# Order of the first key products and the router's transposes, and twelve products ahead of the first layer

## The reference

```python
def _L0_xattn_ref(Q, K, V):                  # Q = layernorm(x), K = V = ctx
    x = einsum('bdn,bdm->bnm', Q, K) / sqrt(dk)
    return einsum('bvn,bnm->bvm', V, sigmoid(x))
def _L0_ffn_ref(h, router_weight, ...):      # h = layernorm(x)
    logits = h @ router_weight.T + router_bias
    # top 4 of 16 experts, softmax; gate_up and down projections of all experts, weighted
def _L3_xattn_ref(h, cond=ctx, ...):         # much later
    kvx = einsum('bsi,oi->bso', cond, w_kv_x)
    kx = _ln(kx.reshape(b, sc, g, d), kxln_w, kxln_b)
x = x + _L0_xattn_ref(_layernorm(x), ctx_2048, ctx_2048)
x = x + _L0_ffn_ref(_layernorm(x), ...)
```

## Time and profile before

| what | value |
|---|---|
| median of 3 runs | 1107.0 us (1106.76 to 1107.4) |
| profiled execution | 1105.54 us |
| its span | 1103.5 us |
| PE busy | 1025.0 us (93%) |
| PEld busy | 869.4 us (79%) |
| DVE busy | 874.6 us (79%) |
| ACT busy | 622.6 us (56%) |
| POOL busy | 567.3 us (51%) |
| mean granted clock of TensorE | 0.986 |

### The profile page before, as it was taken

The page is one execution under the profiler, slowest core; times in us unless marked ns, Lnnn a source line. Parts: engine busy times, 40 slices in busy tenths (PEclk is TensorE's granted clock), DMA queues, the critical chain, the costliest instruction groups (busy, mean ns, idle before and its releaser), DMA issues.

```text
span 1103.5 us, 19047 instructions
## 1 busy us (share of the span) xinstructions
PE 1025.0 (93%) x6546; PEld 869.4 (79%) x6546; DVE 874.6 (79%) x2154; ACT 622.6 (56%) x1657; POOL 567.3 (51%) x412
## 2 busy tenths in 40 slices
PE   6999999999998899888878899999999999999988
PEld 5458888888887686556556888998889988999976
DVE  6448777776778956589999888888887898888885
ACT  1584344444333346677747566666767667765643
POOL 3146666668653243043435665646565475655640
PEclk9999999999999999989979999999999999999999
DMA  7003111110100010100000101010000101000201
GB/s 267 1 1 110 32 55 52 35 59 29 58 1 27 1 56 18 61 1 2 20 1 19 59 1 39 1 58 2 21 19 1 59 1 39 1 20 1 88 1 39
DMA packets 15007, 37.43 MB, mean 34 GB/s; under 512 B 1648, under 2 KB 6848, under 8 KB 14400
## 3 DMA queue, kind: packets, MB, share of 16 engines
q1 hardware_dynamic: 14912, 36.21, 9.7%
HBM read 35.16 MB, written 1.05 MB: 33 GB/s over the span
## 4 chain that ended last, share of the span: by engine, by line
PE 64%; DVE 23%; ACT 6%; issue 4%; POOL 2%; DMA 0%; DVEq 0%; SPq 0%; ACTq 0%; POOLq 0%
PE bank L737 15%; PE bank L759 8%; PE bank L2153 7%; PE bank L2176 7%; PE bank L2084 7%; PE bank L2059 3%; ACT y L2301 3%; PE bank L2095 3%; PE bank L1119 2%; DVE y L286 2%; DVE bst L249 2%; DVE g_ql L2018 2%; PE bank L2073 1%; PE bank L527 1%; DVE arena L1618 1%
## 5 line engine op out<-in xcount | busy, mean ns | idle before, releaser
L2301 ACT ACTIVATE y<-bank,g_mx 128x256 f32<-128x256 f32 x256 | 117.5, 486 | 97.6 <-DVE g_mx L2464 97.6
L2579 POOL TENSOR_TENSOR y<-y,g_sm 128x1024 f32<-128x1024 f32 x64 | 120.2, 1898 | 24.0 <-DVE g_sm L2477 24.0
L2555 POOL TENSOR_TENSOR g_c<-arena 128x1024 fp32r<-128x1024 f32 x30 | 64.1, 2137 | 116.3 <-DVE arena L2398 116.3
L2176 PE MATMUL bank<-arena 128*128 128x256 f32 x512 | 116.0, 379 | 0.0
L788 ACT ACTIVATE arena<-arena 128x512 f32<-128x512 f32 x64 | 40.5, 634 | 120.4 <-DVE arena L873 120.4
L2176 PEld LDWEIGHTS bank<-arena 128*128 128x128 f32 x512 | 94.9, 190 | 12.0 <-issue 0.2
L737 PE MATMUL bank<-b_yh,b_wh 128*128 128x512 f32 x256 | 100.6, 393 | 0.0
L737 PE MATMUL bank<-b_yl,b_wh 128*128 128x512 f32 x256 | 100.0, 391 | 0.0
L737 PE MATMUL bank<-b_yh,b_wl 128*128 128x512 f32 x256 | 99.7, 389 | 0.0
L2059 PE MATMUL bank<-cst,y 128*128 128x128 f32 x512 | 74.0, 277 | 17.7 <-DVE x L2386 14.6
L824 POOL TENSOR_TENSOR b_hl<-arena,b_hh 128x512 fp32r<-128x512 f32 x64 | 81.3, 1292 | 9.6 <-ACT b_hh L797 9.6
(11 more groups left out here) (384 smaller groups left out, 3153.4 us busy)
## 6 DMA issues: line engine op xcount, KB each, us to landing
arena<-in_dram SPq DMA_DIRECT2D x37, 512.0 KB, 3.5
arena<-in_dram SPq DMA_DIRECT2D x18, 256.0 KB, 3.9
arena<-in_dram SPq DMA_DIRECT2D x3, 1024.0 KB, 5.1
arena<-in_dram SPq DMA_DIRECT2D x2, 704.0 KB, 7.0
x<-in_dram SPq DMA_DIRECT2D x4, 256.0 KB, 5.5
cx<-in_dram SPq DMA_DIRECT2D x4, 256.0 KB, 5.6
cxT<-in_dram SPq DMA_DIRECT2D x4, 256.0 KB, 5.8
cx<-in_dram SPq DMA_DIRECT2D x1, 1024.0 KB, 6.1
```

The costliest lines, as they stand in the source:

```text
L2176: m = pe.matmul(o[:, st * 256:st * 256 + 256], g_t[:, c, st * P:st * P + P], keys, start=True, stop=True)
L2301: m = act.activation(g_p[:, c, st, :], o[:, st * 256:st * 256 + 256], ACT.Exp, bias=g_mx[j % 2][:, 2 * c + st:2 * c + st + 1], accum_out=g ...
L2555: pool.tensor_tensor(cat, g_o[j % 2], g_om, ALU.subtract).then_inc(s_gc, 1)
L2579: pool.tensor_tensor(pf, pf, sums, ALU.mult).then_inc(s_gp, 1)
```

## The change

On TensorE, twelve products of `mhalf` with itself (128 by 128 by 128) go into the first quarter of the bank of batch 0's scores, ahead of those scores; nobody reads them, and the scores overwrite them. They wait for `s_pool` to reach 1.

On TensorE at the start of stage B, key product 0 now stands between the transposes of batch 0 and those of batch 1, product 1 between those of batch 1 and batch 2, and the first logits follow the transposes of batch 2. ScalarE's order is changed accordingly. On GpSimd both halves of the key weights are centred in a row, ahead of batch 1's reciprocal root, which stood between them.

```diff
@@ A_pe
                     o = claim(pe, ("A", "s", b))
+                    if b == 0:
+                        pe.wait_ge(s_pool, 1)
+                        for _ in range(12):
+                            pe.matmul(o[:, 0:P], mhalf[:, :], mhalf[:, :], start=True, stop=True)
                     pe.wait_ge(s_ctx[b], 16)
@@ B_pe
-            yt_pe(pe, K_B, "B", range(3))
+            yt_pe(pe, K_B, "B", (0,))
+            K_raw_pe(pe, 0)
+            yt_pe(pe, K_B, "B", (1,))
+            K_raw_pe(pe, 1)
+            yt_pe(pe, K_B, "B", (2,))
             logits(0)
-            K_raw_pe(pe, 0)
-            K_raw_pe(pe, 1)
             yt_pe(pe, K_B, "B", (3,))
@@ B_act
-            yt_act(act, "B", range(3))
+            yt_act(act, "B", range(2))
+            K_raw_act(act, 0)
+            yt_act(act, "B", (2,))
             split_y_act(act, 0)
-            logits(0)
-            K_raw_act(act, 0)
             K_raw_act(act, 1)
             yt_act(act, "B", (3,))
+            logits(0)
+            split_e_act(act, 0)
             K_raw_act(act, 2)
-            split_e_act(act, 0)
             logits(1)
@@ gpsimd
             K_centre_pool(pool, 0)
-            ln_pool(pool, C, K_B, EPS, batches=(1,))
             K_centre_pool(pool, 1)
-            ln_pool(pool, C, K_B, EPS, batches=(2, 3))
+            ln_pool(pool, C, K_B, EPS, batches=(1, 2, 3))
```

## The result

The changed kernel took 1101.47 us (median of 4 runs, 1100.16 to 1102.44), the kernel before 1107.2 us beside it (4 runs, 1106.76 to 1108.79). The ratio is 0.9938, with a 95% interval of 0.9926 to 0.9949; it is not the quotient of these two medians, 0.9948, which lies in that interval. The forecast was 1101.5. Two later comparisons of the same two kernels gave 0.9934 each (0.9921 to 0.9948, and 0.9920 to 0.9948), with the kernel before at 1108.55 and 1108.25 us. The profiled execution took 1100.16 us, with a span of 1098.2 us.

The account below looks back on a forecast made before the run. VectorE was taken to lead until 22.6 us, then TensorE with two pauses and slow logits, then dense TensorE in the experts. Products 0, orders -5.5 us: median 1107.0 to 1101.5 us, range 1098.0 to 1104.6.

Parts of the forecast that it names:

- Part 1: Twelve unread products ahead of the first layer's scores on TensorE: over at 6.1 us, cost 0, gain excluded.
- the 3.6 to 8.2 of the working: Bounds in us for the end of the twelve products ahead of the first scores; 6.1 was taken.
- the rival: Clock falls in the pause after the early scores (8.7 to 10.8): 1.3 us lost, total 1102.8; chance 0.17.
- Part 2: GpSimd's two centrings in a row: VectorE's stall at 25.25 goes, batch 1's y ready 1.17 us earlier.
- the stall of 1.17 us: VectorE's scaling of batch 1 at 25.25, held up by GpSimd's centring: 1.88 - 0.71 = 1.17 us removed.
- Both choices of 0 against a bound of 1.9 us: Beside GpSimd's second centring, VectorE's waiting scaling and its add each lose 0 us, at most 1.9.
- Part 3: New TensorE and ScalarE order before the experts: pauses and slow logits go; with GpSimd's order, 5.51 us saved.
- the two pauses: TensorE waiting for VectorE's y ahead of the transposes at 27.27 and 29.56: 2.17 + 1.66 = 3.83 us, both gone.
- ScalarE's cover: ScalarE empties the banks in time for TensorE, slack 0.6 to 0.9 us; 0.5 us slower per step loses some 1 us.
- The sum of pauses and clock: TensorE ahead of the experts: 3.83 us of pauses plus 1.68 us of logits, 5.51 us; first expert product at 41.5.
- The clock's part: First router logits at the full clock: 1.88 us in place of 3.56, 1.68 us saved.
- Rival five: Clock falls further down, at up to 1.68 us each; four more falls give 1108.2, slower than before; chance 0.04.

Follow-up runs that it names:

- the late products: Changed kernel plus unread products in the last attention layer's pauses (4 at five places, 3 at three): 1100.72 us, ratio 0.9933.
- the smaller centrings: Changed kernel with each of GpSimd's two centring operations cut into two of half the size: 1101.09 us, ratio 0.9935.

## Why the prediction was right

Part 1 stands in the time: the products end at 6.14 (forecast 6.1), and alone they give a ratio of 1.000. Its reason was a little too strong. It let the second scores wait until 10.78 whatever happens, which holds for an x that comes as late as in the profile before; with an early x the slow first scores are what the second ones wait for, and the products bring 0.44 us. That the end met 6.1 so closely is chance: in the eight profiles with these products it lies between 5.29 and 6.47, all inside the 3.6 to 8.2 of the working. The remark that its one effect would be a pause in which the clock can fall is shown too: it happened in one profile of six with the twelve products and no others in the pause (the first one, the two repeats, the products alone, the late products, the smaller centrings), at the price that the rival gave: 1.7 us on TensorE, and 1.32 us at the first transposes (14.18 for 12.86, both with the smaller centrings) where it had 1.3. In the changed kernel itself it did not happen in three profiles.

Part 2: the stall of 1.17 us is gone (0.70 for 1.88; 1.18 by the pause that it shortened in the kernel with GpSimd's order alone), VectorE's scaling got its turn between two queued operations of GpSimd, the add beside a centring cost nothing, and the root was ready in time (24.25, asked for at 24.71). Both choices of 0 against a bound of 1.9 us held. The rule of the Trainium skill ("SBUF — State Buffer", "Who interferes with whom") that a VectorE instruction with at most one SBUF input, outside the two-port modes, does not contend with GpSimd agrees with the add, at 0.67 us beside a centring.

Part 3: the two pauses went to nothing, and ScalarE's cover held; no TensorE row between 22.13 and 40.40 waits for it. The sum of pauses and clock was 5.51 and the stretch shrank by 6.11. The 0.6 us missed is in steps from one start to the next that the sum took as unchanged. The first two groups of transposes take 0.44 us each (23.96 to 24.40, 26.12 to 26.56), where before they ran 0.60 and 0.63 until the pause was counted: 0.35 us. Key product 0 takes 1.72 for 1.82 behind the logits: 0.10. Behind key product 2 the second logits follow after 1.81 for 2.02, where they had waited for ScalarE's copy: 0.21. The other rows take back 0.06. The clock's part is isolated at 1.73 us, for 1.68.

The total was met partly by luck. The lead at the experts was 6.3 to 6.7 us in three profiles, against 47.05, where 5.5 was forecast. For the profiled pair the prediction gave 1100.0 us and a span of 1098.0, and 1100.16 and 1098.2 were measured. That closeness is three misses that nearly cancel: 0.60 us more out of the order and 0.54 us from the earlier arrival of x (0.44 of them with the help of the twelve products), against 1.35 us lost again between 426 and 616 us.

The first comparison gave 5.7 us by the medians, and by the ratios all three gave 6.9 to 7.3, with intervals of 5.6 to 8.9. So 1101.5 met the median, but partly since the kernel before's median was then 1107.2 rather than 1108.3 to 1108.6. Its one profile, at 1105.54, was a fast one: the 49 executions of the kernel before in the later comparisons run from 1105.29 to 1110.24 us, and their mean clocks are mostly 0.980 to 0.983, for 0.986 in that profile. The products-alone kernel shares its work behind the front. Its profile, at a mean clock of 0.981, entered the experts level with the kernel before (47.02 for 47.05) and ended 1.9 us behind it; it took 98.43 us from the third layer's feed-forward to the last attention's values, for 97.35 in that profile. So what the changed kernel's profiles seem to lose behind the experts, 1.3 to 2.8 us, is largely what that one profile of before had not paid. Rival five had the right place: the clock further down decides by about 1 us either way. It did not come near the price of the lead.

Open: whether the 6.9 to 7.3 us of the ratios are more than the 6.11 us of the shorter stretch by chance (their intervals hold it), or by a slightly better meeting of clock and pauses further down. The profiles are one execution each, and no experiment separated this.

## What to carry to other kernels

Read a slow group of matmuls together with the granted clock and with the pauses ahead of it: the pauses cost twice, 3.83 us of waiting and 1.7 us of low clock behind them. Independent work that exists anyway belongs into such pauses; it takes both, while products that nobody reads take only the second. Products ahead of a start that is bound by something else buy next to nothing (0.44 us in an execution in which that something is early, a ratio of 1.000 over twelve), and where they leave a new pause they can cost.

When an engine order is changed, follow the operand of the moved work: here part of the gain on TensorE needed GpSimd's order too (18.30 us from the first transposes to the experts without it, 16.44 with it; the times alone, 5.4 and 6.8 us, have intervals that overlap).

## What the runs showed of the hardware

The clock may or may not fall behind pauses of about the same length. Behind 2.17 and 1.66 us between short transposes it fell in both profiles with that order (the kernel before and the products alone), and behind 0.99 and 1.66 us it held in the one profile. Behind the pause that the early scores leave it fell once in six profiles, and then behind 1.88 us, while it held behind 2.11. The pauses' lengths alone do not say which; with products in the pauses the clock held in each of the three profiles that have them there.

VectorE's scaling waits for GpSimd's centring (the prediction calls it the port). It went on as soon as the one centring that was running ended, though GpSimd had the next one queued behind it. So the size of one GpSimd instruction sets the wait: the pair of scalings took 2.31 us beside centrings of 1024 elements and 1.45 us beside those of 512, for 0.73 without one. Whether GpSimd would get its turn in the same way, waiting for VectorE, no run shows.
